# Two entries of ScalarE's calendar in a Mamba and mixture-of-experts kernel stand later: SiLU of z by four scans, one copy out of PSUM by two

## The reference

```python
def _selective_scan(u, delta, A, Bm, Cm, D):      # per step t, state s of 512 channels x 16
    dA  = jnp.exp(d_t[..., None] * A)
    dBu = d_t[..., None] * B_t[:, None, :] * u_t[..., None]
    s   = dA * s + dBu
    y_t = jnp.einsum('bdn,bn->bd', s, C_t)
    ...
def _mamba(h, ...):
    x_in, z = jnp.split(h @ W_in, 2, axis=-1)
    x_c   = silu(causal_depthwise_conv(x_in, conv_w, conv_b))
    dt, Bm, Cm = jnp.split(x_c @ W_xproj, [64, 80], axis=-1)
    delta = softplus(dt @ W_dt + b_dt)
    y = _selective_scan(x_c, delta, -exp(A_log), Bm, Cm, D_param)
    return (y * silu(z)) @ W_out
# x (8, 1024, 256): x = x + (h + mamba(layernorm(h))), h = layernorm(x)
# then x = x + ffn(layernorm(x)): 8 experts, the best 2 of each row, weighed and added
```

## Time and profile before

| | |
|---|---|
| median of 3 runs | 2350.8 us (2343.01 to 2351.16) |
| the profiled execution | 2349.51 us, of it span 2348.0 us |
| scans of 16 chunks | 41 to 1821 us of the span |
| PE busy | 2161.2 us (92%) |
| DVE busy | 2038.7 us (87%) |
| POOL busy | 1916.6 us (82%) |
| ACT busy | 1661.8 us (71%) |
| granted clock of PE, mean | 0.973 |

### The profile page before, as it was taken

The page is one execution under the profiler, slowest core; times in us unless marked ns, Lnnn a source line. Parts: engine busy times, 40 slices in busy tenths (PEclk is TensorE's granted clock), DMA queues, the critical chain, the costliest instruction groups (busy, mean ns, idle before and its releaser), DMA issues. The chain is left out here.

```text
span 2348.0 us, 45628 instructions
## 1 busy us (share of the span) xinstructions
PE 2161.2 (92%) x13383; PEld 1741.0 (74%) x13383; DVE 2038.7 (87%) x2843; ACT 1661.8 (71%) x3402; POOL 1916.6 (82%) x1207
## 2 busy tenths in 40 slices
PE   8889899999999898989898989999978999999995
PEld 5667777767667776767777776776767889999885
DVE  5899999999999999899999999999999456647776
ACT  6686878778787878777778786877775444445664
POOL 3887989898988989888889898989898466667775
PEclk9999999999999999999999999999998999999998
DMA  6041414232232415050514141313235667657886
GB/s 186 2 154 49 142 51 148 66 125 97 94 121 70 157 43 170 21 170 23 170 33 158 52 144 58 138 65 126 77 105 165 140 112 152 139 96 163 182 181 147
DMA packets 226007, 263.60 MB, mean 112 GB/s; under 512 B 101123, under 2 KB 182563, under 8 KB 225636
## 3 DMA queue, kind: packets, MB, share of 16 engines
q1 hardware_dynamic: 175172, 208.07, 28.8%
q0 software_dynamic: 29904, 34.77, 8.1%
q10 hardware_dynamic: 20688, 17.85, 2.5%
HBM read 196.75 MB, written 71.71 MB: 114 GB/s over the span
## 5 line engine op out<-in xcount | busy, mean ns | idle before, releaser
L893 POOL TENSOR_TENSOR dbu<-drive_u,w_all 128x1024 f32<-128x1024 f32 x384 | 904.2, 2363 | 101.3 <-DVE ps_a L754 46.5
L1172 ACT ACTIVATE ps_a<-delta,a_neg 128x512 f32<-128x512 f32 x768 | 517.2, 685 | 141.1 <-DVE area L754 124.4
L910 POOL TENSOR_TENSOR wp<-area 128x1024 f32<-128x1024 f32 x192 | 453.0, 2359 | 36.8 <-DVE area L754 36.2
L766 DVE TENSOR_TENSOR wd<-ps_a,area 128x1024 f32<-128x1024 f32 x320 | 384.5, 1202 | 0.0
L1436 PEld LDWEIGHTS ps_y<-ident,wd 128*128 128x128 f32 x2560 | 302.5, 144 | 100.0 <-issue 71.1
L1436 PE MATMUL ps_y<-ident,wd 128*128 128x128 f32 x2560 | 341.3, 279 | 13.3 <-DVE wd L766 13.2
L2010 POOL DMA_INDIRECT acc_scratch<-ow,e_meta x135 | 221.7, 1642 | 138.6 <-DVE ow L1928 126.9
L1463 PEld LDWEIGHTS ps_a<-dg,duT 128*128 128x128 f32 x2048 | 252.6, 199 | 67.4 <-issue 64.8
L1463 PE MATMUL ps_a<-dg,duT 128*128 128x128 f32 x2048 | 262.7, 283 | 38.9 <-ACT carry L1179 36.3
L2239 PEld LDWEIGHTS e_ps_h<-xT,w_tile 128*128 128x128 f32 x2160 | 261.4, 193 | 19.6 <-DVE xT L1906 10.1
L2239 PE MATMUL e_ps_h<-xT,w_tile 128*128 128x128 f32 x2160 | 267.4, 277 | 5.2 <-issue 2.9
(11 more groups left out here) (245 smaller groups left out, 3772.0 us busy)
## 6 DMA issues: line engine op xcount, KB each, us to landing
area<-b_scratch SPq DMA_DIRECT2D x128, 512.0 KB, 4.7
w_all<-b_scratch SPq DMA_DIRECT2D x96, 512.0 KB, 4.0
dg<-xs_scratch SPq DMA_DIRECT2D x540, 32.0 KB
area<-in_L_attn_x_dram SPq DMA_DIRECT2D x32, 512.0 KB, 5.0
ee<-acc_scratch SPq DMA_DIRECT2D x32, 512.0 KB, 4.1
x_scratch<-area SPq DMA_DIRECT2D x16, 512.0 KB, 2.9
acc_scratch<-area SPq DMA_DIRECT2D x16, 512.0 KB
area<-x_scratch ACTq DMA_DIRECT2D x32, 256.0 KB
```

The costliest lines, as they stand in the source:

```text
L766: dve.tensor_tensor(wd[:, s % NWD], states(k, 2), cc[:, n:n + 2, :], ALU.mult).then_inc(wd_done, 1)
L893: pool.tensor_tensor(dbu[:, k % NBU], du[:, g % 2, :].unsqueeze(1).broadcast_to([P, 2, CH]), bb[:, row:row + 2, :], ALU.mult).then_inc(dbu ...
L910: pool.tensor_tensor(wp[:, s % 2], ss[:, s % 2], cc[:, rows, :], ALU.mult).then_inc(wp_done, 1)
L1172: act.activation(dst, dl[:, g, :], ACT.Exp, scale=a_neg[:, g, n:n + 1]).then_inc(exp_done, 1)
```

## The change

Two numbers of the calendar. The last number of `x 3` is its lag: ACT's copy stands at step 27 in place of 25. `SILU_Z` is 64 + s: SiLU of z stands at step 13 in place of 9.

```diff
-                  ("out", 1, -1, 16, 2, 6), ("x", 2, 1, 21, 1, 3), ("conv", 0, 1, 22, 1, 2), ("x", 3, 1, 23, 2, 2),
+                  ("out", 1, -1, 16, 2, 6), ("x", 2, 1, 21, 1, 3), ("conv", 0, 1, 22, 1, 2), ("x", 3, 1, 23, 2, 4),
...
-        SILU_Z = 73
+        SILU_Z = 77
```

## The result

The changed kernel takes 2396.21 us (median of 4 runs, 2393.47 to 2400.76), against 2348.3 (4 runs, 2343.01 to 2351.16) for the kernel before: a ratio of 1.0212, with a 95% interval from 1.0194 to 1.0231. The profiled execution took 2397.2 us, of it span 2395.7, 47.7 more than before. The prediction had said 2391.

What follows compares the result with a forecast made beforehand. PE's gapless work ahead of scan 26 was taken to bound the kernel. 2349.5 us + 31.5 (PE's wait for the copy of `out 0`) + 10 (half clock) = 2391 us; range 2366 to 2408 us.

Steps and rivals of the forecast that it cites:

- What bounds the kernel: Scans, chunks 1 to 14: PE's gapless work up to step 46 sets the start of scan 26, not DVE or ACT.
- The SiLU, what it gives: ACT at step 9: work behind comes 1.5 us (even chunks) or 2.3 us (odd) sooner; 3 us of the block was hidden.
- The SiLU, what it costs: PE's `x 1` waits for the copy of `out 0`: 2.5 us in even, 2.0 in odd chunks, 31.5 us in all.
- The price on top: PE's clock falls to half behind the new idle times: six stretches of 1.7 us, 10 us; bounds 0 and 24 us.
- The price of the block: ACT's SiLU block stays 4.53 us; the skill's drain of about 1.38 us a switch, some 38 us, isn't summed.
- The copy of `x 3`: The 2.14 us wait at scan 25 goes and comes back at scan 26 for PE's drive; gain nothing.
- No change: ACT reaches the copy of `out 0` in time, or PE's queue behind it has slack: 2345.5 us; 8%.
- Faster, DVE sets the pace: PE catches up, so DVE's waits for L1143 and exponentials go, less new ones at step 13: 2318 us; 6%.
- The fourth: PE's lateness grows as residual steps (L1062) may miss their rows of x, with all clock losses: 2419 us; 8%.

Runs made afterwards that it cites:

- the first experiment: SiLU of z alone moved to step 13, copy of `x 3` left at step 25, against the kernel before: 2392.53 us, ratio 1.0211.
- the second and fourth experiments: Second: copy of `x 3` alone to step 27, against the kernel before, ratio 1.0004. Fourth: SiLU alone to step 16, against the kernel before, ratio 0.9941.
- the third experiment: The full change plus the copy of `out 0` one step sooner (step 13), ahead of the SiLU block; against the kernel before: 2418.39 us, ratio 1.0306.

## Why the prediction was right

**What bounds the kernel.** Shown: two kernels with DVE waits taken away (the copy of `x 3`, and the drives of group 1) come out at 1.0004 and 1.0013, one with PE's wait added at 1.0211, one with 0.86 us of PE's work less a chunk at 0.9945. The sign to look for was in the earlier trace rows, 73.00 us of PE in 73, and in the end of PE's drive, which lies 0.02 to 0.03 us before scan 26 begins, in each of the chunks 1 to 14.

**The SiLU, what it gives.** As forecast for its size: I had said that 3 us of the block had been hidden, and ACT now idles for 2.68 us ahead of the `keep`; the waits for L1143 are 3.1 us, under the 6 I gave. It has no worth of its own: it is waited out by scan 14 at the latest, 3.0 us late in sum.

**The SiLU, what it costs.** I forecast 2.5 us in an even and 2.0 in an odd chunk, 31.5 in sum. Scan 26 is late by 2.52 (even) and 1.76 us (odd) in the chunks without half clock, 30.0 us over fourteen. The wait at step 13 was forecast at 1.9 and 0.7 us; it is 2.0 and 0.8, and isn't added, as said: it ends at the same scan 26.

**The price on top.** Six half-clock stretches at 1.7 us, 10 us, was the forecast; there are six (chunks 2, 6, 8, 10, 11 and 12) behind the idle time at step 14, and scan 26 is late by 40.0 - 30.0 = 10.0 us more. I had given five to the even chunks and one to the odd, and so it came out, but that the count fits is in part luck. The second trace with the block at step 13 (the first experiment) has four. And the odd chunk is 11, which I hadn't foreseen: ACT waited there for rows of x, 0.78 us ahead of L1062, and that made an idle time of some 1.9 us one of 2.73:

```profile
1312.22 2.08 ACT L1062 ACTIVATE area<-area,nb,sc 128x256 f32<-128x256 f32 x4 [0.78 <-DMA area<-in_L_attn_x_dram]
```

My reason for sparing the odd chunks was also read too narrowly: the shortest idle time that I had counted was 2.09 us, but in the same trace of before the clock fell behind three of 1.85 to 1.96 us too, ahead of L1327 at step 1. The first of them (the granted clock was 0.50 from 265.59 us on):

```profile
264.16 1.14 PE L1327 MATMUL ps_p<-ident,area 128*128 128x128 f32 x8 [1.85 <-ACT area L1114]
```

**What the sum lacked.** The 7.7 us between scans 26 and 42. They are not in any step of mine, for the sum took what stands at scan 26 to be all. At steps 38 and 39 PE's clock falls to half in ten chunks, against five before, and each time scan 42 then waits 1.1 to 1.6 us for its drive; these waits sum to 15.1 us after, 7.8 before. My clock term came out in size for the place it looked at and was blind to the second. With 1.5 us less at the SiLU than forecast (30.0 for 31.5), these 7.7 us are the 6 us by which this execution lies above 2391; the SiLU at 16 gained from the same place. Why the clock falls there in some chunks isn't settled: no run here was made for it.

**The price of the block.** The rows after give 1.28 + 1.92 + 1.28 us, 4.53 from 509.20 to 513.73, as before, and the copy follows at once. The drain of about 1.38 us a switch that the Trainium skill has ("ScalarE: Activation LUTs", What ACT_TABLE_LOAD costs) is not in this trace, so the estimate of 38 us that comes from it was rightly kept out of the sum.

**The copy of `x 3`.** Forecast as nothing; 1.0004 by itself, and on top of the SiLU at 16 nothing again.

**The rivals.** "No change" fell with the 34.7 us at L1333 and the late scan 26. "Faster, DVE sets the pace" fell with the second and fourth experiments. The fourth, residual steps that miss their rows, did occur: L1062 waited for its rows of x two times, 1.0 us in all, in chunks 7 and 11. Where it struck in chunk 11, the fall of the clock came with it.

## What to carry to other kernels

When an engine seems to have waits worth removing, look at the next handover behind them: if the other engine's part of it ends just as the waiting one begins, in every round, then the other sets the pace and the waits are free. Before moving a long block on an engine that has idle time to spare, list what stands behind it up to its next idle time and ask which of it a gapless engine needs; here 4.53 us placed ahead of two copies out of PSUM cost 2%, and the same block behind the two gained 0.5%. In this kernel work taken off the gapless engine came out of the time one for one, and an idle time added to it cost itself and at times the clock.

## What the runs showed of the hardware

In the changed kernel PE's clock fell to 0.50 (1.2 GHz) behind the new idle times of 2.73 to 3.07 us, and behind none of the eight of 1.82 to 2.65 us. The other traces don't keep to these lengths. With half of the SiLU the clock fell behind all five idle times of 2.21 us; with the SiLU's move alone it fell behind one of the five of 2.66 to 2.67 us and not behind the other four; and in the kernel before it had fallen behind idle times from 1.85 us on, though not all. So length alone doesn't tell.

What went with it more closely is what PE's clock had done at steps 1 and 2 of the same chunk. In the three traces in which `x 1` waits behind the block (the changed kernel, the SiLU's move alone, half of the SiLU) there are 21 even chunks. In twelve the clock had stayed full at these steps, and it fell at step 14 in all twelve; in nine it had fallen there, and it fell again at step 14 in one. Within one kernel the nine have the shorter idle times (2.65 for 3.07 us, 1.78 for 2.21), but from one kernel to the other it is the 2.21 us that the fall followed and the 2.65 that it mostly didn't. Behind the 3.38 us of the third experiment it fell in all seven even chunks. What decides is open.

The fall at step 39 came with no idle time at all: PE had been busy throughout, among other things with 16 matmuls of 8 columns each (559.03, 1.95 us), before the stretch from 561.70 to 565.11 at 0.50. The Trainium skill ("TensorE: Matmul & The Clock Gate", Part 1) has the half rate as the default and activity as what releases it. By that alone a busy PE would keep its full rate; the trace doesn't agree at this place, where the rate fell with PE busy in ten of fourteen chunks and stayed full in the other four. No run here tells why.
